# Cross attention in a decoder kernel: weighing last in the slot and two slots behind lowering, the first maximum folded, outputs in slots 8 and 10, the mean on ScalarE

## The chip, the cores and the metric

One core of a Trainium2 chip runs the whole program. The metric is the device time of one execution in microseconds, the median over runs. The engines are called as in the profile: PE (TensorE matmuls), PEld (its weight loads), DVE (VectorE), ACT (ScalarE), POOL (GpSimd), SP (SyncE).

## The reference

The program is a two-layer decoder. The change is in one of its six parts, the cross attention of layer 1, and that part computes, for 4 rows (batch entries) of 256 tokens:

```python
q = rms_norm((x @ Wq.T) as 16 heads of 128, q_norm_w)             # 256 queries
kv_in = concat([context (1601), x (256)])
k = rms_norm((kv_in @ Wk.T) as 4 heads of 128, k_norm_w)
v = (kv_in @ Wv.T) as 4 heads of 128
q, k = rope(q, positions of x), rope(k, all positions)
probs = softmax(q @ k.T / sqrt(128))                               # 4 query heads share a key head
x = x + (probs @ v) @ Wo.T
```

The norm is `w * (x * rsqrt(mean(x*x) + 1e-6))`. The mean in it, the maximum in the softmax and the product of the probabilities with v are what the change moves.

## The kernel before, in words

`cross_attention` prepares the normed tokens and constants (stage cross_w) and then calls `cross_stream`, in which every engine walks through the same list of numbered **slots** (`SLOTS`, L1755) and in each slot issues what an order written out by hand gives it. The engines meet only by semaphores, so an engine may run ahead or behind, and within an engine everything is in order.

The work has 4 rows x 4 key heads = 16 **groups**; each has 2 **passes** (half of the 4 query heads that share the key head: 512 columns = 2 heads x 256 queries). A pass has `STEPS` = 15 **steps**, one for each tile of 128 keys (the last has 65). So there are 32 passes and 480 steps, and step s starts in slot s. A group is 30 slots. One step goes through these stages:

- slot s: PE `score` (L1947, three bf16 matmuls of high and low parts into bank 0 or 1), ACT `copy_scores` (L2036) into a tile in memory called a room, DVE `keep_most` (L2203 for the first tile of a pass, L2206 for the others), which keeps the running maximum `most`. `score` of step s waits for `keep_most` of step s-2, whose bank it reuses.
- at the end of a pass: PE `turn_most` (L1955) transposes the maxima into bank 6, DVE `take_top` (L2212) reduces them, PE `turn_top` (L1961) turns them, ACT `flatten` (L2076) negates, PE `spread` (L1968) spreads them over bank 7. They stand in slots 0, 1 and 2 of the next pass (`TOPS_LATE`, `FLAT_LATE`, `SPREAD_LATE`); take_top in slot 0.
- slot s+18 (`LOWER`): DVE `lower` (L2194) adds the negated maximum, ACT `exponent` (L2042) takes exp.
- slot s+19 (`WEIGH`): PE `weigh` (L1979, one fp32 matmul seen as two instructions) multiplies with v, directly behind the slot's score; POOL `accumulate` (L2133, L2136) adds up the row sums. The room is free after both. There are 21 rooms (`ROOMS`), and `copy_scores` waits for the weighing and the sum of step s-21.
- after a pass: ACT `att_high` (L2082) and, a slot later, DVE `att_low` (L2248) split the result; PE `sum_up` (L1986) sums over partitions into bank 6, DVE `invert` (L2254) takes the reciprocal; PE `project_out` (L2000) multiplies each of the pass's two heads with Wo into bank 6, and DVE `add_out` (L2265) adds to x.

Counted modulo 15, a pass's att_high is in slot 4, att_low and sum_up in slot 5, and the two outputs in slots 6 and 9. In the last pass both outputs stand in one slot and in other banks.

Beside the steps run the projections for the next group, in 96 **units**, one every 5 slots (`EVERY`): 2 query units (128 queries of 4 heads) and 4 key units (up to 4 tiles) a group. From a unit's start slot: PE `project` (L1892) in slots 0 to 3 (a query unit in 0 and 1); ACT `square` (L2052) and, for key units, `take_values` (L2060) in slots 2 and 4; DVE `rotate` (L2233, L2234) in slots 3 and 6, and behind it `vary` (L2240), which makes the mean of the squares plus 1e-6; POOL `add_up` (L2143) in slot 6 and `normalise` (L2149, L2154) in slot 7; PE `turn` (L1934) in slot 9 transposes into bank 6; ACT `high` (L2070) in that slot and DVE `low` (L2244) in the next split the result. Modulo 15, turns stand in slots 2, 7 and 12.

Bank 6 is shared by turn_most, turn_top, turn, sum_up and project_out, in the order of the slots; `bank6_before` (L1835) makes each wait for the semaphore of the one before it: the reducing, flattening, low part, reciprocal or add. 

In three groups (1, 5, 9) the angles of the next row are made: DVE L2313 to L2319 in six slots from slot 29 to slot 4, ACT `waves` (L1628 to L1630, with table loads) behind slot 11. Around groups 3, 7 and 11 the next row's context is split (ACT L2117, DVE L2323) and POOL makes tables (L1608, L1609). The others are called plain groups here.

## Time and profile before

| | us |
|---|---|
| median of 3 runs | 1730.97 |
| lowest and highest | 1723.27, 1736.09 |
| the profiled execution's own time | 1732.53 |
| its span, first to last instruction | 1730.7 |
| of it, scores of slot 0 to slot 479 | 460.1 to 1601.6 |

The granted clock over the span is 0.953 of full speed. Slots 0 to 479 are two thirds of the span. Busy time in the tables below is a union: matmuls are pipelined, and the next begins before the one before it has ended in the record.

### The profile page before, as it was taken

The page shows a single profiled execution, that of the slowest core. Times are in us where ns is not written, and L with a number is a line of the kernel's source. Part 1 is how long each engine was busy: PE and PEld are TensorE (multiplying, and loading weights), DVE is VectorE, ACT ScalarE, POOL GpSimd, SP SyncE. Part 2 cuts the span into 40 slices and gives each one's busy share as a digit, 9 for nine tenths or more (in the row PEclk, how much of TensorE's full clock was granted, in tenths as well). Part 3 has the DMA queues.
Part 4 walks back from the last instruction along what each step waited for, and adds up shares of the span by engine and source line. Part 5 has one row for each costly group of instructions (what it writes and reads, how often), then busy time and mean ns, then how long its engine had stood idle before and what let it go on. Part 6 is the DMA issues. An engine that isn't in the chain of part 4 may idle for free. (4 is left out here: it accounts for less than half of the span.)

```text
span 1730.7 us, 26027 instructions
## 1 busy us (share of the span) xinstructions
PE 1517.4 (88%) x8324; PEld 878.2 (51%) x8324; DVE 1338.3 (77%) x2706; ACT 1014.7 (59%) x2343; POOL 1147.3 (66%) x1068
## 2 busy tenths in 40 slices
PE   6597796766798999999899999989989999999697
PEld 5476464533454554545455454545545555454354
DVE  7875577878687888888788878878887888888554
ACT  3363564652566666666666666666656666666342
POOL 2363470132577789888688977867998777886542
PEclk9799798879899999999999999999999999999889
DMA  3000820010000001000000000000000000000010
GB/s 97 1 2 13 303 88 25 1 70 0 32 13 1 13 13 39 1 1 1 1 1 13 27 1 1 1 1 1 21 19 1 1 1 1 1 1 1 7 49 26
DMA packets 30945, 38.49 MB, mean 22 GB/s; under 512 B 4948, under 2 KB 26456, under 8 KB 30808
## 3 DMA queue, kind: packets, MB, share of 16 engines
q1 hardware_dynamic: 30808, 36.82, 6.6%
q8 instruction: 67, 1.10, 0.3%
q14 instruction: 70, 0.57, 0.1%
HBM read 35.76 MB, written 1.05 MB: 21 GB/s over the span
## 5 line engine op out<-in xcount | busy, mean ns | idle before, releaser
L2136 POOL TENSOR_TENSOR stream_acc<-stream_acc,stream_weights 128x512 f32<-128x512 f32 (+1 forms) x404 | 523.6, 1296 | 135.6 <-ACT stream_weights L2042 119.8
L1979 PE MATMUL stream_banks<-stream_weights,stream_v 128*128 128x512 f32 (+1 forms) x872 | 458.8, 610 | 37.3 <-ACT stream_weights L2042 36.3
L2036 ACT COPY stream_weights<-stream_banks 128x512 f32<-128x512 f32 (+1 forms) x436 | 256.5, 588 | 263.3 <-PE stream_banks L1947 260.1
L2206 DVE TENSOR_TENSOR stream_most<-stream_most,stream_banks 128x512 f32<-128x512 f32 x448 | 304.9, 681 | 79.4 <-ACT stream_weights L2036 71.9
L2042 ACT ACTIVATE stream_weights<-stream_weights 128x512 f32<-128x512 f32 (+1 forms) x436 | 277.0, 636 | 110.4 <-DVE stream_weights L2194 107.6
L2194 DVE TENSOR_TENSOR stream_weights<-stream_weights,stream_banks 128x512 f32<-128x512 f32 (+1 forms) x436 | 295.1, 679 | 3.2 <-PE stream_banks L1968 1.8
L1979 PEld LDWEIGHTS stream_banks<-stream_weights,stream_v 128*128 128x128 f32 (+1 forms) x872 | 159.1, 191 | 132.6 <-ACT stream_weights L2042 81.9
L1947 PE MATMUL stream_banks<-stream_q_t_hi,stream_k_t_hi 128*128 128x512 bf16 (+1 forms) x480 | 183.6, 383 | 9.9 <-DVE stream_most L2206 8.6
L1947 PE MATMUL stream_banks<-stream_q_t_lo,stream_k_t_hi 128*128 128x512 bf16 (+1 forms) x480 | 183.1, 381 | 0.0
L1947 PE MATMUL stream_banks<-stream_q_t_hi,stream_k_t_lo 128*128 128x512 bf16 (+1 forms) x480 | 183.0, 381 | 0.0
L2143 POOL TENSOR_TENSOR stream_by_cos<-stream_by_cos,stream_by_sin 128x256 f32<-128x256 f32 x192 | 135.0, 725 | 50.0 <-DVE stream_by_sin L2234 49.8
L2154 POOL TENSOR_TENSOR stream_normed<-stream_by_cos,stream_rms 128x512 f32<-128x512 f32 x96 | 96.9, 1009 | 7.5
L2052 ACT ACTIVATE stream_squares<-stream_banks 128x128 bf16<-128x128 f32 x368 | 95.8, 270 | 10.1 <-PE stream_banks L1892 10.1
L2149 POOL TENSOR_TENSOR stream_rms<-stream_var,cross_half 128x4 f32<-128x4 f32 x96 | 101.4, 1056 | 0.0
L1892 PEld LDWEIGHTS stream_banks<-early_w_kv_hi,row_in_t_hi 128*128 128x128 bf16 x416 | 39.3, 98 | 88.0 <-issue 85.1
L1892 PE MATMUL stream_banks<-early_w_kv_hi,row_in_t_hi 128*128 128x256 bf16 x416 | 79.6, 273 | 0.6 <-DVE stream_by_sin L2234 0.6
L1892 PE MATMUL stream_banks<-early_w_kv_hi,row_in_t_lo 128*128 128x256 bf16 x416 | 79.4, 273 | 0.0
L1892 PE MATMUL stream_banks<-early_w_kv_lo,row_in_t_hi 128*128 128x256 bf16 x416 | 79.4, 272 | 0.0
L2265 DVE SCALAR_TENSOR_TENSOR model_x<-stream_banks,stream_inv,model_x 128x256 f32<-128x256 f32 x128 | 55.9, 477 | 28.4 <-PE stream_banks L2000 28.4
L1947 PEld LDWEIGHTS stream_banks<-stream_q_t_hi,stream_k_t_lo 128*128 128x128 bf16 (+1 forms) x480 | 47.6, 99 | 57.1 <-issue 1.5
L1934 PE MATMUL stream_banks<-model_ident,stream_normed 128*128 128x128 f32 x368 | 59.0, 282 | 20.0 <-DVE model_x L2265 18.5
L2052 ACT ACTIVATION_READ_ACCUMULATOR stream_squares<-stream_banks 128x1 f32 x368 | 75.0, 204 | 0.0
(436 smaller groups left out, 3114.3 us busy)
## 6 DMA issues: line engine op xcount, KB each, us to landing
memory_raw_t<-in_ctx_t SPq DMA_DIRECT2D x4, 1601.0 KB, 9.0
memory_raw<-in_ctx SPq DMA_DIRECT2D x4, 1536.0 KB
row_ctx_t<-in_ctx_t SPq DMA_DIRECT2D x6, 512.0 KB, 3.6
early_raw<-in_L_xattn_Wq SPq DMA_DIRECT2D x4, 512.0 KB, 3.9
early_raw<-in_L_xattn_Wo SPq DMA_DIRECT2D x4, 512.0 KB, 3.9
row_ctx_t<-in_ctx_t SPq DMA_DIRECT2D x1, 1601.0 KB, 8.0
moe_raw_up<-in_L_ffn_wi SPq DMA_DIRECT2D x6, 256.0 KB, 4.3
model_x<-in_x SPq DMA_DIRECT2D x1, 1024.0 KB, 5.5
```

The lines of the kernel that those rows point to most:

```text
L1892: last = nc.tensor.matmul(out, rows, moving(two, c), start=(n == 0), stop=(n == 3 * DC - 1))
L1947: last = nc.tensor.matmul(ps[0:r, step % 2, :], k_t[one][:, t * P:t * P + r], q_t[two][:, g % 2, PAIR * n:PAIR * (n + 1), :], start=(one = ...
L1979: nc.tensor.matmul(ps[:, 2 + n, :], v[0:r, g % 2, t, :], room(step)[0:r], start=(t == 0), stop=(t == KT - 1)).then_inc(weighed, 1)
L2036: nc.scalar.copy(room(step)[0:r], ps[0:r, step % 2, :]).then_inc(copied, 1)
L2042: nc.scalar.activation(room(step)[0:r], room(step)[0:r], ACT.Exp, scale=SCALE).then_inc(p_ready, 1)
L2052: last = nc.scalar.activation(squares[:, h, :], heads[:, h - some.start, :], ACT.Square, accum_out=ss[:, u % 2, h:h + 1])
L2136: nc.gpsimd.tensor_tensor(acc[0:r, h % 2, :], acc[0:r, h % 2, :], room(step)[0:r], ALU.add).then_inc(acc_ready, 1)
L2143: last = nc.gpsimd.tensor_tensor(by_cos[:, u % 2, 0:n, to], by_cos[:, u % 2, 0:n, to], by_sin[:, u % 2, 0:n, of], ALU.add)
L2149: nc.gpsimd.tensor_tensor(rms[:, u % 2, 0:n], var[:, u % 2, 0:n], half[:, 0:n], ALU.pow).then_inc(rms_ready, 1)
L2154: nc.gpsimd.tensor_tensor(normed[:, 0:n], by_cos[:, u % 2, 0:n], bcast(rms[:, u % 2, 0:n], 2, HD), ALU.mult).then_inc(normed_ready, 1)
L2194: nc.vector.tensor_tensor(room(step)[0:r], room(step)[0:r], ps[0:r, 7, :], ALU.add).then_inc(lowered, 1)
L2206: nc.vector.tensor_tensor(most[0:r], most[0:r], ps[0:r, step % 2, :], ALU.max).then_inc(maxed, 1)
```

## The change

WEIGH goes from LOWER + 1 to LOWER + 2 and ROOMS from 21 to 22. The room is made by laying the small tiles ss, var, rms, inv and flat into the unused end of `ctx_t`. On PE, the projection moves ahead of the top's steps and the weighing to the slot's end. On DVE, the first maximum of a pass is taken together with the second, from the room of the first tile (`maxima` counts the semaphore), the score of the third tile waits for the copy instead of the maximum, and take_top moves one slot on and ahead of the slot's maximum. Outputs stand in slots 8 and 10 of a pass; att_high, att_low and the sum move one slot on with WEIGH. The mean moves from DVE to ACT.

```diff
 LOWER = STEPS + 3
-WEIGH = LOWER + 1
-ROOMS = 21
+WEIGH = LOWER + 2
+ROOMS = 22
 def rows_of(tile):
...
 SUM_LATE = ATT_LATE + 1
+OUT_LATE = 2 * STEPS + 8
 def outs_in(slot):
...
     for m in range(PAIR):
-        found += [(h, m) for h in pass_at(slot, SUM_LATE + (1, 4)[m]) if h < PASSES - 1]
+        found += [(h, m) for h in pass_at(slot, OUT_LATE + 2 * m) if h < PASSES - 1]
         found += [(h, m) for h in pass_at(slot, SUM_LATE + 1) if h == PASSES - 1]
...
+        eps = sb("eps", [P, 1])
...
+                    nc.gpsimd.memset(eps[:], 1e-6)
                 @block.scalar
...
         v = sb("v", [P, 2, KT, HD])
-        ss = sb("ss", [P, 2, 4])
-        var = sb("var", [P, 2, 4])
-        rms = sb("rms", [P, 2, 4])
         by_cos = sb("by_cos", [P, 2, 4, HD])
         by_sin = sb("by_sin", [P, 2, 4, HD])
-        flat = sb("flat", [4, P], BF16)
         acc = sb("acc", [P, 2, HALF])
-        inv = sb("inv", [P, REP * QT])
         att = [sb(f"att_{part}", [P, PAIR, SEQ], BF16) for part in ("hi", "lo")]
         spare = ctx_t[:].rearrange("p c n -> p (c n)")
+        ss, var, rms = (spare[:, DC * CTX + 8 * i - 64:DC * CTX + 8 * i - 56].rearrange("p (u n) -> p u n", u=2) for i in range(3))
+        inv = spare[:, DC * CTX - 8:DC * CTX]
+        flat = spare[0:4, DC * CTX - 128:DC * CTX - 64].bitcast(BF16)
         SPARE_ROOMS = DC * CTX // HALF - 4
...
             return h, h // HALVES, h % HALVES, t
+
+        def maxima(step):
+
+            return step - step // STEPS
         def room(step):
...
                         pe.wait_ge(lo_ready, UNITS * g + QT + t // 4 + 1)
-                    if step >= 2:
-                        pe.wait_ge(maxed, step - 1)
+                    if step >= 2 and (step - 2) % STEPS == 0:
+                        pe.wait_ge(copied, step - 1)
+                    elif step >= 2:
+                        pe.wait_ge(maxed, maxima(step - 2))
                     else:
...
                 def turn_most(h):
-                    pe.wait_ge(maxed, STEPS * (h + 1))
+                    pe.wait_ge(maxed, maxima(STEPS * (h + 1) - 1))
                     wait_bank6("tops", h)
...
                     for c in range(4):
-                        last = nc.tensor.matmul(ps[:, 7, c * P:(c + 1) * P], own[:, c, :], flat[:], start=True, stop=True)
+                        last = nc.tensor.matmul(ps[:, 7, c * P:(c + 1) * P], own[:, c, :], flat, start=True, stop=True)
                     last.then_inc(spread_ready, 1)
...
                         score(slot)
-                    if 0 <= slot - WEIGH < ALL:
-                        weigh(slot - WEIGH)
+                    for e in range(4):
+                        for u in units_at(slot, e):
+                            project(u, e)
                     for h in pass_at(slot, TOPS_LATE):
...
                         spread(h)
-                    for e in range(4):
-                        for u in units_at(slot, e):
-                            project(u, e)
                     for u in turns_in(slot):
...
                         project_out(h, m)
+                    if 0 <= slot - WEIGH < ALL:
+                        weigh(slot - WEIGH)
             @block.scalar
...
                     last.then_inc(squared, 1)
+                def vary(u, n):
+                    heads = slice(0, width(u))
+                    if u >= 2:
+                        ac.wait_ge(rms_ready, u - 1)
+                    ac.wait_ge(squared, part_at[(u, n)] + 1)
+                    nc.scalar.activation(var[:, u % 2, heads], ss[:, u % 2, heads], ACT.Identity, bias=eps[:, 0:1],
+                                         scale=1.0 / HD).then_inc(var_ready, 1)
+
                 def take_values(u, n):
...
                         ac.wait_ge(spread_ready, h)
-                    nc.scalar.mul(flat[:], ps[0:4, 6, 0:P], -1.0).then_inc(flat_ready, 1)
+                    nc.scalar.mul(flat, ps[0:4, 6, 0:P], -1.0).then_inc(flat_ready, 1)
                 def att_high(h):
...
                             take_values(u, 0)
+                        else:
+                            vary(u, 0)
                     for u in units_at(slot, 4):
...
                             take_values(u, 1)
+                            vary(u, 1)
                     for h in pass_at(slot, FLAT_LATE):
...
                     r = rows_of(t)
+                    if t == 0:
+                        return
                     ve.wait_ge(copied, step + 1)
-                    if t == 0:
+                    if t == 1:
                         if h >= 1:
                             ve.wait_ge(most_turned, h)
-                        nc.vector.tensor_copy(most[:], ps[:, step % 2, :]).then_inc(maxed, 1)
+                        nc.vector.tensor_tensor(most[:], room(step - 1), ps[:, step % 2, :], ALU.max).then_inc(maxed, 1)
                     else:
-                        ve.wait_ge(maxed, step)
+                        ve.wait_ge(maxed, maxima(step - 1))
                         nc.vector.tensor_tensor(most[0:r], most[0:r], ps[0:r, step % 2, :], ALU.max).then_inc(maxed, 1)
...
                     nc.vector.tensor_tensor(by_sin[:, u % 2, some], heads, tab[1], ALU.mult).then_inc(taken, 1)
-                def vary(u):
-                    n = width(u)
-                    if u >= 2:
-                        ve.wait_ge(rms_ready, u - 1)
-                    nc.vector.tensor_scalar(var[:, u % 2, 0:n], ss[:, u % 2, 0:n], 1.0 / HD, 1e-6, ALU.mult, ALU.add).then_inc(var_ready, 1)
-
                 def low(u):
...
                         rotate(u, 0)
-                        if unit(u)[1] < QT:
-                            vary(u)
                     for u in units_at(slot, 6):
...
                             rotate(u, 1)
-                            vary(u)
+                    for h in pass_at(slot, TOPS_LATE + 1):
+                        take_top(h)
                     if 0 <= slot < ALL:
                         keep_most(slot)
-                    for h in pass_at(slot, TOPS_LATE):
-                        take_top(h)
                     for h in pass_at(slot, SUM_LATE):
...
```

## Rows read from the trace of the kernel before

**Rows 1.** The page's first part: busy time by engine.

```profile
PE 1517.4 (88%) x8324; PEld 878.2 (51%) x8324; DVE 1338.3 (77%) x2706; ACT 1014.7 (59%) x2343; POOL 1147.3 (66%) x1068
```

**Rows 2.** Windows by group: length, busy time (count) per engine, clock, DMA.

```profile
460.00:593.00 133.00, 117.84 (x575) 63.76 (x574) 106.29 (x192) 88.59 (x231) 95.13 (x92) 0.97 0.03 9
...
1036.00:1107.00 71.00, 68.49 (x335) 37.65 (x334) 57.94 (x108) 45.66 (x124) 57.42 (x56) 1.00 0.00 1
1107.00:1187.00 80.00, 71.05 (x334) 38.46 (x333) 63.61 (x114) 51.18 (x129) 61.57 (x56) 0.96 0.00 1
...
1257.00:1333.00 76.00, 70.94 (x340) 38.44 (x338) 62.13 (x112) 46.69 (x126) 64.93 (x66) 0.98 0.04 11
...
1545.00:1602.00 57.00, 53.48 (x217) 25.45 (x216) 47.63 (x82) 37.71 (x73) 40.84 (x36) 1.00 0.00 1
```

**Rows 3.** Waits of PE, 600 to 1600 us: total us, times, longest.

```profile
PE stream_banks L1979 <- ACT stream_weights L2042: 25.4, 39, 4.0
PE stream_banks L1934 <- DVE model_x L2265: 17.3, 13, 2.0
```

**Rows 4.** Timeline, slots 0 and 1 of a plain group.

```profile
1035.56 0.38 PE L1947 MATMUL stream_banks<-stream_q_t_hi,stream_k_t_hi 128*128 128x512 bf16 x1
...
1036.41 0.58 ACT L2036 COPY stream_weights<-stream_banks 128x512 f32<-128x512 f32 x1 [1.05 <-PE stream_banks L1947]
...
1037.07 0.60 PE L1955 MATMUL stream_banks<-model_ident,stream_most 128*128 128x128 f32 x4
1037.42 0.27 ACT L2052 ACTIVATE stream_squares<-stream_banks 128x128 bf16<-128x128 f32 x1
...
1037.77 0.69 DVE L2203 COPY stream_most<-stream_banks 128x512 f32<-128x512 f32 x1 [1.41 <-PE stream_banks L1955]
...
1037.92 0.38 ACT L2060 COPY stream_v<-stream_banks 128x256 f32<-128x256 f32 x1
...
1038.16 0.38 PE L1947 MATMUL stream_banks<-stream_q_t_hi,stream_k_t_hi 128*128 128x512 bf16 x1
...
1039.57 0.42 DVE L2233 TENSOR_TENSOR stream_by_cos<-stream_banks,row_k_tab_cos 128x256 f32<-128x256 f32 x1
...
1039.76 0.22 PE L1961 MATMUL stream_banks<-model_ident_b,stream_top 128*4 128x128 bf16 x1
```

**Rows 5.** Timeline, slots 6 and 7 of that group.

```profile
1050.08 0.69 DVE L2233 TENSOR_TENSOR stream_by_cos<-stream_banks,row_q_tab_cos 128x512 f32<-128x512 f32 x1
...
1051.28 1.17 DVE L2240 TENSOR_SCALAR stream_var<-stream_ss 128x4 f32<-128x4 f32 x1
...
1052.97 0.86 DVE L2265 SCALAR_TENSOR_TENSOR model_x<-stream_banks,stream_inv,model_x 128x256 f32<-128x256 f32 x2
...
1053.98 0.52 PE L1934 MATMUL stream_banks<-model_ident,stream_normed 128*128 128x128 f32 x3 [1.07 <-DVE model_x L2265]
```

**Rows 6.** Timeline, slots 11 to 13 of a group that turns angles.

```profile
1138.56 1.28 ACT L1628 ACT_TABLE_LOAD   x1
...
1144.66 0.63 ACT L2042 ACTIVATE stream_weights<-stream_weights 128x512 f32<-128x512 f32 x1
...
1145.34 2.07 PE L1979 MATMUL stream_banks<-stream_weights,stream_v 128*128 128x512 f32 x2 [3.97 <-ACT stream_weights L2042]
```

**Rows 7.** One line's instructions: ns min/median/max, forms.

```profile
L2240 DVE TENSOR_SCALAR stream_var<-stream_ss x96: 153/160/1180, 445.5 to 1554.5; 128x4 f32<-128x4 f32 x80, 128x3 f32<-128x3 f32 x16
```

**Rows 8.** Groups by line: shapes, busy us, mean ns, idle before.

```profile
L2070 ACT CAST stream_k_t_hi<-stream_banks 128x512 bf16<-128x512 f32 x64 | 36.2, 565 | 2.4 <-PE stream_banks L1934 1.3
L2082 ACT CAST stream_att_hi<-stream_banks 128x512 bf16<-128x512 f32 x32 | 18.4, 575 | 3.0 <-PE stream_banks L1979 3.0
L2248 DVE TENSOR_TENSOR stream_att_lo<-stream_banks,stream_att_hi 128x512 bf16<-128x512 f32 x32 | 21.9, 684 | 4.9 <-ACT stream_att_hi L2082 4.9
...
L1671 ACT ACTIVATE cross_w_rs<-cross_w_rs 128x8 f32<-128x8 f32 x1 | 0.2, 209 | 0.0
L2254 DVE RECIPROCAL stream_inv<-stream_banks 128x4 f32<-128x4 f32 x32 | 5.8, 182 | 22.8 <-PE stream_banks L1986 22.8
```

More of the change, by code:

```diff
@@ L1702, in _, with cross_stream @@
                                                 own_t[0][:, :, tok], ALU.subtract)
-        cross_stream(nc, x, const, a, w, experts, w_q, w_kv, w_o, k_gain, q_gain, freq, ones, own, half, own_t, in_t, ctx_t,
+        cross_stream(nc, x, const, a, w, experts, w_q, w_kv, w_o, k_gain, q_gain, freq, ones, own, half, eps, own_t, in_t, ctx_t,
                      where, where_f, angle, turns, sin, k_tab, q_tab, kept["raw"])
-def cross_stream(nc, x, const, a, w, experts, w_q, w_kv, w_o, k_gain, q_gain, freq, ones, own, half, own_t, in_t, ctx_t,
+def cross_stream(nc, x, const, a, w, experts, w_q, w_kv, w_o, k_gain, q_gain, freq, ones, own, half, eps, own_t, in_t, ctx_t,
                  where, where_f, angle, turns, sin, k_tab, q_tab, raw):
```

## The prediction

> **What bounds the kernel now.** The page's engine totals come first: PE 88%, DVE 77%, POOL 66%, ACT 59% [rows 1]. The share of PE hides the stage that the change touches, so the second view is the table of windows, one for each group of 30 slots [rows 2]. A plain group (eight of groups 1 to 14; its windows are all like 1036 to 1107) takes 71.0 us and PE is busy in 68.49 of them. Groups 1, 5 and 9, in which the next row's angles are made, take 80 us with 71.05 busy; groups 3, 7 and 11, in which the next context is split, 76 with 70.94. So PE is the bound, and what can be won is its idle time. The third view, PE's waits from 600 to 1600 us, says where it is: 25.4 us before the weighing matmul for ACT's exponent, and 17.3 us, 13 times, before the turning transposes for DVE's add into x [rows 3].
>
> Idle time understates a stall. A score matmul is shown as 0.38 us long though the next starts 0.22 later, so each stall first swallows about 0.16 us of tail. In the timeline I took each slot's length less its matmuls at their steady pace. Of a plain group's 71.0 us that leaves 3.7: 1.25 in slot 7 (the turn waits for the add of the output in slot 6; 1.07 of it shows as idle [rows 5]), 0.25 in slot 8, 0.3, 1.1 and 0.7 in slots 11 to 13 (weighing waits for the exponent, the score for the maximum) and 0.1 in slot 2. Slots 14 to 29 lose nothing. The cause in slots 6 to 13 is DVE: query units cost it two full-width products, and then the mean of the squares, a 128x4 instruction whose median is 160 ns and whose longest is 1180 [rows 7]. In slot 6 it takes 1.17 [rows 5]; I found it at 0.9 to 1.2 for nearly all query units after the first four.
>
> The Trainium skill (SBUF — State Buffer, Who interferes with whom) says that a DVE tensor_scalar between SBUF tiles can need the port pair that it shares with GpSimd, and then blocks until GpSimd's instruction ends, while ScalarE never waits on anyone. The trace agrees: the 1.17 us instruction ends as POOL's sum does. By that rule the long means vanish on ACT; without it each could cost ACT up to the 1.18 of DVE, 2 us more for a group's two query units.
>
> **The change, part by part.** I work in one plain group, in us from a slot's start. Fixed points, from slots 0 and 1 [rows 4]: the copy of scores starts 0.85 after the score and ends at 1.43; two squares take 0.50; after the copy, the exponent and two squares, the values are copied from 2.36 to 2.74; first transpose of the maxima to DVE's start 0.70. DVE instructions of 0.68 follow each other at 0.60, and PE starts about 0.15 after the DVE result it needs (add's end 1053.83, turn 1053.98 [rows 5]). PE's steady pieces: score 0.65, weighing 0.86, projection 0.65, four transposes 0.44, output 0.65, row sums 0.81.
>
> 1. Weighing last and one slot later. The exponent is then done two slots ahead, so the waits of the weighing go in every plain slot. What is late next is the maximum that the score two slots on needs: its earliest end is 2.15 and it is wanted after two slots (3.0 at least). The 22nd tile keeps the copy's distance to the weighing and to POOL's sum that it reuses at two slots, so it costs nothing; POOL's sum also gets its exponent earlier.
>
> 2. The mean on ACT. DVE loses 1.15 twice a group and 0.16 four times. ACT gains six instructions; the nearest row, 128x8, has 209 ns [rows 8], so I take 0.2 each, 20 us over the stage on an engine that is 64% busy in a plain group. Bounds: below nothing can't be; above, the 1.18 of DVE's longest. The Trainium skill (ScalarE: Activation LUTs, What ACT_TABLE_LOAD costs) prices an instruction with a column as bias at 280 ns instead; by it the wait in slot 7 below grows by 0.07, 1 us over the stage.
>
> 3. First maximum folded. One 0.69 copy less on DVE in each of 32 passes; it also waited 1.41 for the transposes [rows 4]. With 2 this removes the stalls of slots 11 to 13: adding up DVE's queue from slot 6, the maximum of slot 11 ends 0.2 before score 13 asks for it, that of slot 12 over 1 before. Gain 2.1, and 0.1 in slot 2.
>
> 4. take_top now stands in slot 1, behind rotate. New wait: rotate needs the values, copied at 2.74, that is 0.15 into slot 1. It then takes 0.75 (its products start 0.34 apart, the second lasts 0.41), take_top starts at 3.45 and ends at 4.13, and turn_top can start at 4.3. PE is there at 3.25 in slot 1 (no projection) and at 3.9 in slot 16. Queued behind it on PE are the weighing and the next score, so it is paid: 1.05 and 0.35. Least nothing, if PE trails; at most 1.2 more each, if DVE also has an angle instruction in front.
>
> 5. Outputs in slots 8 and 10. The turn in slot 7 waits no longer for an add, saving 1.25 and the 0.25 after it. It now waits for the reciprocal behind the row sums of slot 6. Before that stand, on ACT from slot 5: copy, exponent, the attention cast (0.58, now in slot 5 [rows 8]), four squares, mean, which holds copy 6 until 3.6. On DVE: two products to 4.8, maximum 6 to 5.4, reciprocal (0.18 [rows 8]) to 5.5. PE is there at 4.5: new wait 1.15. The output in slot 8 follows the low part of turn 7 by 0.2 and does not wait. In slot 23 it does: in ACT's slot 22 stand two squares, values and the mean ahead of the high part (0.57 [rows 8]), which ends 1.5 into slot 23; the low part ends at 2.2, and PE is at the output at 1.3: new wait 0.95.
>
> Plain stalls: old 3.7 gone, new 1.05 + 0.35 + 1.15 + 0.95 = 3.5. Net -0.15 in each of 14 groups: -2 us. The four waits could each be nothing or twice as long: 3.5 a group either way, 49 us, the widest bound of all.
>
> 6. Angle groups. ACT is away for its table loads and three waves from 1138.56, and the next exponent starts at 1144.66; PE weighed only at 1145.34, after 3.97 idle [rows 6], and the granted clock of that window is 0.96 against 1.00 of a plain one [rows 2]. Now this weighing needs nothing from that slot. What is late is copy 12, 6.8 after slot 11 starts, so maximum 12 ends at 7.5 and score 14, due at 5.6, waits 1.9; score 15 waits 0.85. Old extra 5.9, new 2.8 with 0.8 for a clock that may fall again: -2.3. In slots 1 to 7, where DVE has about six angle instructions besides, old extra 2.8, new 1.3: about -2.7 with group 1, the longest, counted in. -5 in each of three groups: -15 us. From nothing (the wait only moves to the score) to -9 (all their excess over 71).
>
> 7. Context groups. The old extra of 4.4 sits in slots 2, 7 and 8, behind DVE's split of 1.6; the split of slot 0 now falls where DVE idles, that of slot 5 lengthens the wait in slot 7 by 1.3. I take off 1 more for POOL, which has tables to make besides. -2 each, -6 us; from 0 to -4.4 each.
>
> 8. First group: PE is idle 15.2 in 460 to 593, of which 9 belong to group 1; of the other 6, the first weighing's wait, with the shorter DVE queue, gives -2.5. Last group: 3.5 idle [rows 2], slots without projection, where weighing waits most: -2.5. One more weighing in the drain I set against a maximum turned earlier: 0, within 1.5 either way.
>
> Sum: -2 - 15 - 6 - 2.5 - 2.5 = -28. The profiled execution took 1732.53 (span 1730.7 and 1.8 around it): 1704.5. It lies 1.6 above the median of 1730.97, so 1703.
>
> **The rivals.** (a) The old waits go and the new ones are half as long, because ACT and DVE run ahead once the means are gone: 1.75 x 14 = 25 more, 1678. For it: slots 16 to 29 had slack everywhere. Against: the four waits are chains, not queues. (b) The long stalls of the row changes only move, from the weighing to the score: parts 6 and 7 nothing, 1703 + 21 = 1724, within 1%. For it: ACT's 6 us absence stays. Against: the score has two slots of reserve. (c) Slower: bank 6 changes hands through ACT with one slot less. If ACT holds each mean until its own squares are through, and the high part, the values and the next copy queue behind it, every new wait grows. At 2 us more for a group it eats the 28; at 3.3 more (0.8 on each wait, within the bound of 3.5) the time is 1703 + 46 = 1749. Against: ACT's 45.66 us in a plain group of 71. (d) The extra slot of weighing does nothing, since PE was bound by throughput: only parts 2 and 3 count, and the time is as in (b).
>
> **How the numbers follow.** A measurement of this kernel can tell about 1% (17 us) from no change. Forecast, 1690 to 1714: 0.45. (a): 0.18. (b) with (d): 0.24. (c): 0.13. Faster by over 1% is the forecast and (a): 0.63; within 1%: (b), (d) and the milder part of (c), 0.27; slower: 0.10. The range leaves out about a tenth on each side: 1676 to 1738.
>
> **What would show it.** In a plain group: PE's wait for the exponent near nothing; new PE waits for the top maxima (slots 1, 16), for the reciprocal at the turn (slot 7), for the low part at the output (slot 23), about 1 us each; DVE busy about 4 us less than its 57.94; the mean on ACT near 0.2 with no table load beside it; plain groups still at 70 to 71.5, angle groups at 75. Wrong if plain groups fall below 69 (a), if they rise above 73 (c), or if angle groups stay at 80 (b).

## The result and the profile after

The changed kernel takes 1703.81 us, median of 4 runs (1701.68 to 1704.56), against 1731.08 (1723.27 to 1736.09): a ratio of 0.9846, 95% interval 0.9813 to 0.9879. The forecast was 1703. So the time is right; whether its terms are is another matter, and most of what follows is about terms that were wrong and cancelled. One execution of the kernel before, timed with b_outs below, took 5358.82 us and is left out of the median there.

The page's first part answers to [rows 1] (some 110 matmul records are missing in this trace, so PE's busy time is a little low). DVE lost 56 us, ACT gained 15. In the plain window below DVE is busy 3.0 us less than before (54.90 for 57.94), where the forecast had about 4.

```profile
PE 1481.1 (87%) x8215; PEld 854.0 (50%) x8324; DVE 1282.7 (75%) x2578; ACT 1029.3 (60%) x2439; POOL 1146.3 (67%) x1069
```

The windows by group, for the same stretches as [rows 2]: groups 0 and 1, a plain one, one with angles, one with a context split, the last; and, as a sixth, the experts' stage. Columns as there.

```profile
460.00:588.00 128.00, 114.98 (x566) 60.85 (x574) 101.74 (x176) 90.15 (x240) 93.51 (x91) 0.99 0.03 9
1023.00:1094.00 71.00, 67.68 (x333) 36.65 (x337) 54.90 (x102) 46.65 (x131) 58.12 (x56) 1.00 0.00 1
1094.00:1170.00 76.00, 67.26 (x327) 36.00 (x331) 59.96 (x104) 52.09 (x135) 60.34 (x56) 1.00 0.00 1
1241.00:1314.00 73.00, 67.15 (x324) 35.65 (x329) 56.29 (x100) 46.83 (x131) 63.76 (x65) 1.00 0.04 12
1526.00:1581.00 55.00, 52.05 (x210) 25.09 (x212) 46.05 (x79) 37.30 (x74) 42.39 (x38) 1.00 0.00 1
1618.00:1702.80 84.80, 72.07 (x424) 41.57 (x432) 46.57 (x126) 31.00 (x53) 28.22 (x25) 0.96 0.13 41
```

Windows have rounded ends. Measured from the score copy that opens one group to the one that opens the next, the plain groups before took 70.5 to 71.5 us and now take 70.5 or 70.6 (forecast -0.15 each, measured -0.3 on average). Groups 1, 5 and 9 fell from 80.5, 80.3 and 80.1 to 76.6, 76.3 and 76.2 (forecast -5, measured -3.9). Of the context groups, 7 and 11 fell by 1.8, and 3 did not (73.5 to 74.0; forecast -2 each). First and last group: -1.5 each (forecast -2.5). From the first score copy to the last that is 20.6 us, where the terms of the forecast give 28.

**PE's clock differed too.** Between the first score copy and the last, the kernel before ran for 30.7 us at the lower of the two clock levels (1.2 GHz of 2.4), all of it in groups 1, 5 and 9 (6.8 each) and 3, 7 and 11 (3.4 each); the changed kernel ran for 3.4 us at it, in group 1. That is the granted clock of 0.96 and 0.98 in [rows 2] against 1.00 above. In group 9 of the kernel before it fell at 1143.4, within the 3.97 us of idle time of [rows 6], and rose at 1150.2. What such a stretch costs can be read from groups 5 and 9, which run the same instructions. In the experiment u_mean below, group 5 had 6.8 us at the lower level and took 78.4 us, group 9 had none and took 76.5 (granted clock 0.96 and 1.00 in their windows):

```profile
795.50:873.90 78.40, 71.29 (x334) 37.13 (x333) 63.21 (x112) 51.27 (x130) 61.61 (x57) 0.96 0.00 1
1087.30:1163.80 76.50, 68.20 (x336) 36.14 (x334) 62.88 (x113) 51.21 (x130) 62.65 (x57) 1.00 0.00 1
```

Between the same two groups, 3.4 us more at the lower level go with 1.2 us more time in u_lag, with 0.5 in u_order and with none in o_top. By these (0 to 0.35 us for each us) the clock's share of the 20.6 can be anything up to 9.7 us; this is an estimate, and no run separates it.

PE's waits from 580 to 1580 us answer to [rows 3] (in this window the kernel before has 24.8 for the exponent, in 38 times, and 17.3 for the add): what PE waited for, us in total, times, longest. The waits for the exponent and for the add are gone, and three new ones stand in their place.

```profile
PE stream_banks L1968 <- DVE stream_top L2232: 20.4, 28, 1.4
PE stream_banks L1939 <- DVE row_ctx_t L2268: 15.7, 13, 1.7
PE stream_banks L2007 <- DVE stream_k_t_lo L2258: 11.2, 14, 1.2
PE stream_banks L1954 <- DVE stream_most L2226: 6.3, 5, 2.0
PE stream_banks L1939 <- POOL stream_normed L2172: 4.0, 6, 0.9
PE stream_banks L1975 <- DVE stream_weights L2212: 2.1, 2, 1.1
```

In the timeline of plain group 12 they are, in order, the top maxima in slot 1, the reciprocal at the turn of slot 7 (the place of the add in [rows 5]), the top maxima in slot 16 and the low part at the output of slot 23. The last column is the idle time: 1.03, 0.92, 0.27, 0.78, where the forecast had 1.05, 1.15, 0.35 and 0.95. The forecast counted a stall with the 0.16 us of tail that it swallows first; in that measure they are 1.19, 1.08, 0.43 and 0.94, together 3.6 for 3.5.

```profile
1317.79 0.22 PE L1968 MATMUL stream_banks<-model_ident_b,stream_top 128*4 128x128 bf16 x1 [1.03 <-DVE stream_top L2232]
...
1331.26 0.52 PE L1939 MATMUL stream_banks<-model_ident,stream_normed 128*128 128x128 f32 x3 [0.92 <-DVE row_ctx_t L2268]
...
1351.71 0.22 PE L1968 MATMUL stream_banks<-model_ident_b,stream_top 128*4 128x128 bf16 x1 [0.27 <-DVE stream_top L2232]
...
1368.98 0.28 PE L2007 MATMUL stream_banks<-cross_w_o_hi,stream_att_hi 128*128 128x256 bf16 x1 [0.78 <-DVE stream_k_t_lo L2258]
```

The mean on ACT, one line's instructions (ns min/median/max), against [rows 7]:

```profile
L2067 ACT ACTIVATE row_ctx_t<-row_ctx_t,cross_eps x96: 297/306/328, 443.6 to 1532.6; 128x4 f32<-128x4 f32 x80, 128x3 f32<-128x3 f32 x16
```

**Where the other 7 us are.** Span fell by 27.9, the stream's 480 slots by 20.6. From the last score copy to PE's last work of the stage it took 34.9 before and 31.5 now: -3.4, in the drain, which the forecast had at 0. And from the experts' first matmul to the end it took 87.8 and now 84.4, with no instruction changed there: -3.4 at a granted clock of 0.96 in the window above, against 0.90 in the kernel before in a window with the same 432 matmuls (it begins 2.9 us ahead of the first):

```profile
1640.00:1730.70 90.70, 76.84 (x432) 43.28 (x432) 47.42 (x137) 32.48 (x55) 28.19 (x25) 0.90 0.13 39
```

### The profile page after: what moved, and what is told of

Read it like the earlier page. It is cut to its first block and busy times, and to the rows that moved or that the text cites. A ratio compares the mean times of both kernels' runs of the same rounds, so it can differ in the third digit from the quotient of the medians.

```text
span 1702.8 us, 25942 instructions
## 1 busy us (share of the span) xinstructions
PE 1481.1 (87%) x8215; PEld 854.0 (50%) x8324; DVE 1282.7 (75%) x2578; ACT 1029.3 (60%) x2439; POOL 1146.3 (67%) x1069
## 3 DMA queue, kind: packets, MB, share of 16 engines
HBM read 35.76 MB, written 1.05 MB: 22 GB/s over the span
## 5 line engine op out<-in xcount | busy, mean ns | idle before, releaser
L1986 PE MATMUL stream_banks<-stream_weights,stream_v 128*128 128x512 f32 (+1 forms) x876 | 452.0, 600 | 0.0
L2226 DVE TENSOR_TENSOR stream_most<-stream_most,stream_banks 128x512 f32<-128x512 f32 (+1 forms) x416 | 283.9, 683 | 160.4 <-ACT stream_weights L2043 143.9
L1954 PE MATMUL stream_banks<-stream_q_t_hi,stream_k_t_hi 128*128 128x512 bf16 (+1 forms) x390 | 148.0, 379 | 10.2 <-DVE stream_most L2226 10.0
L1986 PEld LDWEIGHTS stream_banks<-stream_weights,stream_v 128*128 128x128 f32 (+1 forms) x876 | 139.7, 191 | 22.9 <-issue 5.3
L1954 PEld LDWEIGHTS stream_banks<-stream_q_t_lo,stream_k_t_hi 128*128 128x128 bf16 (+1 forms) x480 | 47.4, 99 | 148.0 <-issue 145.8
L1954 PEld LDWEIGHTS stream_banks<-stream_q_t_hi,stream_k_t_hi 128*128 128x128 bf16 (+1 forms) x480 | 47.3, 99 | 132.0 <-issue 96.7
L2172 POOL TENSOR_TENSOR stream_normed<-stream_by_cos,row_ctx_t 128x512 f32<-128x512 f32 x96 | 100.1, 1043 | 7.5
L2167 POOL TENSOR_TENSOR row_ctx_t<-row_ctx_t,cross_half 128x4 f32<-128x4 f32 x96 | 95.4, 993 | 0.0
L2253 DVE TENSOR_TENSOR stream_by_cos<-stream_banks,row_k_tab_cos 128x256 f32<-128x256 f32 (+1 forms) x128 | 51.4, 402 | 40.1 <-ACT stream_squares L2059 25.1
```

The source lines that it names most:

```text
L1954: last = nc.tensor.matmul(ps[0:r, step % 2, :], k_t[one][:, t * P:t * P + r], q_t[two][:, g % 2, PAIR * n:PAIR * (n + 1), :], start=(one = ...
L1986: nc.tensor.matmul(ps[:, 2 + n, :], v[0:r, g % 2, t, :], room(step)[0:r], start=(t == 0), stop=(t == KT - 1)).then_inc(weighed, 1)
L2167: nc.gpsimd.tensor_tensor(rms[:, u % 2, 0:n], var[:, u % 2, 0:n], half[:, 0:n], ALU.pow).then_inc(rms_ready, 1)
L2172: nc.gpsimd.tensor_tensor(normed[:, 0:n], by_cos[:, u % 2, 0:n], bcast(rms[:, u % 2, 0:n], 2, HD), ALU.mult).then_inc(normed_ready, 1)
L2226: nc.vector.tensor_tensor(most[0:r], most[0:r], ps[0:r, step % 2, :], ALU.max).then_inc(maxed, 1)
```

## The experiments

All were timed against the kernel before, whose medians lay between 1730.8 and 1732.2 in these sets. Six edits can be taken apart: PE's order, the lag with its tile, the mean, the fold, take_top's slot and the outputs' slots.

### First set: one part of the change undone

**u_mean**: the mean back on DVE, behind the products.

```diff
-                    ac.wait_ge(squared, part_at[(u, n)] + 1)
-                    nc.scalar.activation(var[:, u % 2, heads], ss[:, u % 2, heads], ACT.Identity, bias=eps[:, 0:1],
+                    nc.vector.tensor_scalar(var[:, u % 2, 0:n], ss[:, u % 2, 0:n], 1.0 / HD, 1e-6, ALU.mult, ALU.add)
```

> The changed kernel with the mean back on DVE behind rotate, all else kept. Theory (chains of waits per slot): the mean of a query unit takes 1.15 us there again. In slot 7 the reciprocal comes 1.0 later, so the turn's wait grows from 1.2 to 2.2; the maximum of slot 11 ends 0.9 after score 13 asks for it; slot 23 wins 0.3 on ACT. +1.65 in each of 15 groups: about 1728 us. Rival (only the weighing's distance matters, DVE's queue is off the path): 1703 to 1707.

Measured: 1714.40 us, ratio 0.9907 (0.9890 to 0.9923). The mean's move is worth 10.6, in size between the theory and its rival. A plain group grows by 0.6: slot 13 by 0.62, slot 7 by 0.20, and slot 23 is 0.19 shorter. The theory took every query unit's mean at 1.15 us; back on DVE, 20 of the 96 means took over 0.6 us, where the kernel before had 34.

**u_lag**: one slot of lag and 21 rooms, weighing still last.

```diff
-WEIGH = LOWER + 2
-ROOMS = 22
+WEIGH = LOWER + 1
+ROOMS = 21
```

> The changed kernel with WEIGH = LOWER + 1 and ROOMS = 21, weighing still last in the slot. Theory: last in the slot, the weighing finds its exponent done in a plain group even one slot behind; angle groups lose about 1 us each. The cast of the attention and the row sums go back to slots 4 and 5, so the reciprocal is there before turn 7: that wait of 1.2 falls to 0, and the output in slot 8 waits 0.15. About -10 us in all: 1694. Rival (the distance of two slots is what brought the gain): the exponent's waits come back, 1718 to 1728.

Measured: 1705.43, ratio 0.9851 (0.9834 to 0.9867): no difference from the changed kernel (the intervals overlap), and neither the theory nor its rival. The trace shows two effects that cancel. Plain groups are shorter, 69.6 or 69.7 for 70.5, as the row sums fall one slot earlier and the turn of slot 7 finds the reciprocal done. Groups 1, 5 and 9 are longer by 1.7 to 3.3. PE's waits from 580 to 1580 us in u_lag: the reciprocal is absent, and the exponent is back three times: 4.11 us at 838.93 and at 1130.02, behind ACT's waves in groups 5 and 9, and 1.30 in the last group. Ahead of this window it is back in group 1 too, with 4.11 at 547.23.

```profile
PE stream_banks L1968 <- DVE stream_top L2232: 19.4, 27, 1.4
PE stream_banks L2007 <- DVE stream_k_t_lo L2258: 13.3, 19, 1.1
PE stream_banks L1986 <- ACT stream_weights L2049: 9.5, 3, 4.1
PE stream_banks L1939 <- POOL stream_normed L2172: 7.3, 11, 1.0
```

**u_order**: PE's old order (weighing behind the score, projections behind the spread); everything else as changed.

```diff
                         score(slot)
+                    if 0 <= slot - WEIGH < ALL:
+                        weigh(slot - WEIGH)
...
                         spread(h)
+                    for e in range(4):
+                        for u in units_at(slot, e):
+                            project(u, e)
```

> The changed kernel with PE's old order in a slot (weighing right behind the score, projection behind the top's steps), distance two kept. Theory: the exponent is done two slots ahead, so the weighing waits nowhere, and its 0.86 us now covers the waits behind it: turn_top in slots 1 and 16 (1.05 and 0.35 to 0.2 each), turn in slot 7 (1.2 to 0.3), output in slot 23 (0.95 to 0.1). -2.5 to -3 in each of 15 groups: about 1662 us. Rival (weighing last is a part of the gain, since it lets the score's followers start early): 1710 to 1730.

Measured: 1674.92, ratio 0.9679 (0.9663 to 0.9696). PE's new order, the first thing the change does, costs 29 us; the theory had 42. The three new waits shrink from 20.4, 15.7 and 11.2 to 8.9, 9.2 and 0.6. The edit moves the projections as well as the weighing. In slots 1 and 7 there is no projection, and in slot 23 it is ahead of the output in both orders, so in these three only the place of the weighing differs. PE's waits from 580 to 1580 in u_order (the 4.7 us for POOL's sum lie behind the last score, in the drain):

```profile
PE stream_banks L1939 <- DVE row_ctx_t L2268: 9.2, 11, 1.8
PE stream_banks L1968 <- DVE stream_top L2232: 8.9, 14, 1.4
PE stream_banks L1993 <- POOL stream_acc L2154: 4.7, 1, 4.7
...
PE stream_banks L2007 <- DVE stream_k_t_lo L2258: 0.6, 2, 0.4
```

Its timeline in slot 1 shows why: the score, then the weighing of 0.86, and behind it turn_top has only 0.18 left to wait, where it waited 1.03 when it stood right behind the score.

```profile
1293.98 0.38 PE L1954 MATMUL stream_banks<-stream_q_t_hi,stream_k_t_lo 128*128 128x512 bf16 x1
1294.19 1.02 PE L1986 MATMUL stream_banks<-stream_weights,stream_v 128*128 128x512 f32 x2
1295.39 0.22 PE L1968 MATMUL stream_banks<-model_ident_b,stream_top 128*4 128x128 bf16 x1 [0.18 <-DVE stream_top L2232]
```

**a_top**: take_top back in the slot of the transposes, behind the maximum.

```diff
-                    for h in pass_at(slot, TOPS_LATE + 1):
-                        take_top(h)
                     if 0 <= slot < ALL:
                         keep_most(slot)
+                    for h in pass_at(slot, TOPS_LATE):
+                        take_top(h)
```

> The changed kernel with take_top back in slot 0, behind where the maximum stands. Theory: it can start 2.0 after slot 0 begins, ends at 2.7, and turn_top, due at 3.25 and 3.9, waits no more: slot 1 shorter by 1.05, slot 16 by 0.35; spread then waits up to 0.5 in slot 2 for the last lowering. -0.9 in each of 15 groups: about 1690 us. Rival (these waits only move to the next slots, whose chain through ACT and DVE is as long): 1702 to 1705.

Measured: 1696.24, ratio 0.9805 (0.9787 to 0.9824): 7.6 less than the changed kernel. The 20.4 us of PE's wait for the top maxima are gone, and 11.6 us of a wait of the spread for the lowering have come (2.1 in the changed kernel). In a plain group slots 1 and 16 lose 0.99 and 0.33; slot 2 gains 0.29: -1.0, a little more than the theory's 0.9. The time misses the theory's 1690 by 6 in the groups with angles: groups 5 and 9 take 78.0 for 76.3, with a wait of 2.6 for the lowering in slot 2 and 6.8 us at the lower clock, where the changed kernel has none.

### Second set

**u_fold**: the first maximum as a copy of its own again, in the changed kernel.

```diff
-                    if t == 0:
-                        return
-                    if t == 1:
+                    if t == 0:
...
-                        nc.vector.tensor_tensor(most[:], room(step - 1), ps[:, step % 2, :], ALU.max).then_inc(maxed, 1)
+                        nc.vector.tensor_copy(most[:], ps[:, step % 2, :]).then_inc(maxed, 1)
```

> The changed kernel (1703.8) with the fold alone undone: the first maximum of each pass is again a copy of its own (0.69 us of DVE in each of 32 passes, behind PE's transposes of the maxima). Theory, from the forecast: DVE is behind after the query units, and the copy it no longer saves gives back part of the stalls of slots 11 to 14. With the mean back on DVE (u_mean) that stall was 0.6 to 0.8 us a group; the fold saves less of DVE's time per group in the same slots, so about 0.8 us x 14 = 11 us more, 1715. Rival, the copy is hidden (it ran while DVE waited for the transposes anyway, and the mean on ACT has already cleared slots 11 to 14): 1702 to 1706.

Measured: 1725.9, median of 10 runs, ratio 0.9972 (0.9956 to 0.9988). The fold is worth 22 us, twice what I thought and in another place: slots 11 to 14 stay as they were in plain groups, and the loss is in slots 1 and 16 (2.74 to 3.11 each), and in the groups with angles, which take 77.8 to 80.8 for 76.2 to 76.6 (groups 1 and 5, the long ones, with 6.8 and 10.2 us at the lower clock, group 9 with none). PE's wait for the top maxima goes from 20.4 to 35.0, longest 2.7. DVE's timeline in slots 0 and 1 has no gap between the copy and take_top (L2228): the copy waits 1.10 for the transposes, and lowering, both products and take_top queue behind it.

```profile
1328.47 0.69 DVE L2219 COPY stream_most<-stream_banks 128x512 f32<-128x512 f32 x1 [1.10 <-PE stream_banks L1960]
1329.08 0.68 DVE L2210 TENSOR_TENSOR stream_weights<-stream_weights,stream_banks 128x512 f32<-128x512 f32 x1
1329.67 0.42 DVE L2249 TENSOR_TENSOR stream_by_cos<-stream_banks,row_k_tab_cos 128x256 f32<-128x256 f32 x1
1330.01 0.41 DVE L2250 TENSOR_TENSOR stream_by_sin<-stream_banks,row_k_tab_sin 128x256 f32<-128x256 f32 x1
1330.34 0.68 DVE L2228 TENSOR_REDUCE stream_top<-stream_banks 128x4 bf16<-128x512 f32 x1
```

**a_outs**: outputs in slots 9 and 10.

```diff
-OUT_LATE = 2 * STEPS + 8
+OUT_LATE = 2 * STEPS + 9
...
-        found += [(h, m) for h in pass_at(slot, OUT_LATE + 2 * m) if h < PASSES - 1]
+        found += [(h, m) for h in pass_at(slot, OUT_LATE + m) if h < PASSES - 1]
```

> The changed kernel (1703.8) with the outputs in slots 9 and 10 instead of 8 and 10, so the second pass's first output stands in slot 24 instead of 23. Theory: PE's wait of 11.2 us in 14 times for the low part at the output of slot 23 goes, and nothing takes its place, as slot 24's output finds the low part long done: 1703.8 - 11 = 1693. In the trace that wait is near zero. Rival: two adds of the output in neighbouring slots put DVE behind, and the wait turns into one of the score for the maximum or of slot 11: 1702 to 1706.

Measured: 1692.9, ratio 0.9781 (0.9755 to 0.9807), as the theory says. The wait for the low part at the output is no longer among PE's waits; nearly every group between the first and the last loses 1.0 and nothing takes its place.

**o_top**: u_order and a_top together (both diffs above).

> The changed kernel with PE's old order (u_order, 1674.9) and, besides, take_top back in the slot of the transposes. Theory: the two edits add up only as far as u_order still waits for the top maxima, 8.9 us in 14 times; the spread takes back 0.3 a group: 1674.9 - 8.9 + 4 = 1670. Rival, the edits are independent and take_top gives the 7.6 it gave in the new order: 1667. Second rival, the wait only moves to the spread, since the old order leaves DVE's queue as it is: 1674 to 1676.

Measured: 1668.04 (1667.55 to 1668.33), ratio 0.9643 (0.9619 to 0.9668), between the theory and the first rival. It is the fastest of all kernels here, 63 us under the kernel before. A plain group is down to 67.2 us, and PE is busy in 66.85 of a window of 67 (with [rows 2]: 68.49 of 71.0):

```profile
1000.00:1067.00 67.00, 66.85 (x333) 37.91 (x332) 53.55 (x98) 46.22 (x129) 56.02 (x55) 1.00 0.00 1
```

**o_lag1**: u_order and u_lag together.

> The changed kernel with PE's old order and the old lag of one slot and 21 tiles: what is left of the change is the mean on ACT, the fold, outputs 8 and 10 and take_top in slot 1. Theory: in a plain group the exponent is now early enough through the shorter DVE queue, and the row sums fall in slot 5, so that the turn of slot 7 no longer waits for the reciprocal (u_lag showed 0.9 us a group from that): -0.9 x 11 = -10; the angle groups lose what the lag gave, 2 to 3 us each: +9. 1673 to 1676, as u_order. Rival, the lag is what removed the waits for the exponent: they come back as 20 of the 27 us that the kernel before showed: 1695.

Measured: 1699.53, ratio 0.9819 (0.9791 to 0.9847): the rival, and 4.5 beyond it. In PE's old order the second slot of lag is worth 24.6 us, in the new order 1.6. PE's first wait from 580 to 1580 is the exponent again, against 0.8 us in u_order:

```profile
PE stream_banks L1986 <- ACT stream_weights L2049: 21.0, 27, 4.5
```

### Third and fourth set: one part alone

**b_outs**: the kernel before with the outputs in slots 8 and 10 alone. **b_lag**: the same with the second slot of lag and the 22nd tile. **b_order**: b_outs with PE's new order. In all three the small tiles already lie in `ctx_t`, as in the changed kernel.

```diff
 b_outs, b_lag, b_order
-        found += [(h, m) for h in pass_at(slot, SUM_LATE + (1, 4)[m]) if h < PASSES - 1]
+        found += [(h, m) for h in pass_at(slot, OUT_LATE + 2 * m) if h < PASSES - 1]
 b_lag
-WEIGH = LOWER + 1
-ROOMS = 21
+WEIGH = LOWER + 2
+ROOMS = 22
 b_order
-                    if 0 <= slot - WEIGH < ALL:
-                        weigh(slot - WEIGH)
...
                         project_out(h, m)
+                    if 0 <= slot - WEIGH < ALL:
+                        weigh(slot - WEIGH)
```

> The kernel before (1731.4) with the outputs in slots 8 and 10 alone; lag, PE's order, mean, copy and take_top as before. Against b_lag (1682.8) it has one slot of lag less. Theory, the gain of b_lag is the sum of two: PE's wait of 17.3 us for the output's add at the turn of slot 7 goes here, with the 0.25 of a group behind it, about 18 to 20 us: 1712, and the other 29 are the lag's. Rival, the lag is worth only the 24.6 that stood between o_lag1 and u_order: 1707. Second rival, the outputs pay nothing with one slot of lag, since DVE's queue is as long and the weighing waits for the exponent instead: 1725 to 1731.

Measured: 1713.95, ratio 0.9904 (0.9877 to 0.9930): against the 1730.79 of this set the outputs are worth 16.8, near the theory. PE's wait for the add is gone; its waits for the exponent (28.9 us in 42 times) and of the score for the maximum (9.3) are 4 us longer each than in the kernel before.

> The kernel before (1731.4) with the second slot of lag and the 22nd tile, and the outputs in slots 8 and 10 that this needs; PE's order, the mean on DVE, the first maximum's copy and take_top in slot 0 as before. Theory, the lag pays by itself in the old order: between u_order and o_lag1 (both with mean and fold) it was worth 24.6, and the parts add up: 1674.9 + 10.6 (mean) + 22.1 (fold) - 6.9 (take_top) = 1700.7. Rival, the lag pays only once DVE's queue is short: without mean and fold the maximum is late too, the score waits where the weighing waited, and the time is 1715 or more. Third: the fold's 22 hangs on take_top in slot 1, and without it this kernel is at 1680 to 1690.

Measured: 1682.78, ratio 0.9726 (0.9690 to 0.9763): the third expectation. Outputs and lag alone give 49 of the 63 us of the best kernel. PE no longer waits for the exponent (1.2 us), and the score waits for the maximum instead, 13.1 us in 14 times. Mean and fold together add 14.7 to this (o_top), where undoing them one by one in the changed kernel cost 10.6 and 22.1.

> The kernel before (1731.4) with PE's new order (projections ahead, weighing last) and the outputs in slots 8 and 10, the lag still one slot; mean, copy of the first maximum and take_top as before. Theory, weighing last only costs once the exponent's wait is paid by either way: in this kernel it removes the exponent's waits as the lag would, and brings the new waits of the short transposes: parts added from the changed kernel, 1703.8 + 1.6 (lag) + 10.6 (mean) + 22.1 (fold) - 7.6 (take_top) = 1730.5, no change. Rival, the cost of 29 us of the new order stands by itself and nothing is won: 1755. Other rival, less work of DVE in the wrong place matters only with take_top in slot 1: 1708 to 1715.

Measured: 1710.01, ratio 0.9877 (0.9835 to 0.9918): the second rival's range; the theory, which added up parts measured around the changed kernel, was 20 us too high. Between b_outs (1713.95) and this there are 3.9 us, and the intervals overlap: with one slot of lag, weighing last does remove most of the exponent's waits (28.9 to 9.1), and its price takes nearly all of it back (spread 3.0 to 16.3, low part at the output 0.5 to 13.6).

**o_top_inv**: o_top with the reciprocal ahead of DVE's products and maximum.

```diff
+                    for h in pass_at(slot, SUM_LATE):
+                        invert(h)
                     for u in units_at(slot, 3):
                         rotate(u, 0)
...
-                    for h in pass_at(slot, SUM_LATE):
-                        invert(h)
```

> The best so far (o_top, 1668.0: old order, take_top in slot 0, all else as in the changed kernel) with the reciprocal of the row sums ahead of the two products and the maximum in DVE's slot. Theory: PE's 8.1 us in 13 waits for the reciprocal at the turn of slot 7 are its place in DVE's queue, so they go, and what is late next there is small: 1661. Rival, DVE then waits for the row sums with the products queued behind it, and the maximum is later by as much: 1666 to 1670.

Measured: 1682.78, ratio 0.9722 (0.9684 to 0.9761): 14.7 worse than o_top, worse than the rival too. The reciprocal's wait is gone from PE's list, as the theory said, but the score and the output now wait:

```profile
PE stream_banks L1954 <- DVE stream_most L2226: 14.9, 17, 2.1
PE stream_banks L2007 <- DVE stream_k_t_lo L2258: 12.6, 13, 1.0
```

DVE itself waits for the row sums 30.3 us in 24 times, where in o_top, in whose slots the products and the maximum came first, it was 12.1 in 12. DVE's waits from 580 to 1580 us, o_top_inv and then o_top:

```profile
DVE row_ctx_t L2268 <- PE stream_banks L1993: 30.3, 24, 2.0
```

```profile
DVE row_ctx_t L2268 <- PE stream_banks L1993: 12.1, 12, 5.4
```

## Why the forecast was right, and where it was not

The sum was right. What the parts are worth in it can be read along one chain of runs, each one step from its neighbour: outputs in slots 8 and 10 (kernel before to b_outs) -16.8, second slot of lag (to b_lag) -31.2, mean and fold (to o_top) -14.7, take_top in slot 1 (to u_order) +6.9, PE's new order (to the changed kernel) +28.9. The change is 63 us of gain and 36 of loss. In another sequence the parts have other sizes, as the steps below show. By its own steps:

1. **Weighing last and one slot later.** "The waits of the weighing go in every plain slot": right. The step failed in taking two edits as one and the order as free. They do the same thing: PE's waits for the exponent go from 28.9 to 1.2 by the lag alone (b_lag) and to 9.1 by the order alone (b_order). With the old order the lag is worth 24.6 us (o_lag1 to u_order), or 31.2 with mean, first maximum and take_top as before (b_outs to b_lag). With the weighing last it is worth 1.6, within the noise. The order's price of 29 us was in the forecast (as most of 3.5 us a group), but under other names: as the new waits of steps 4 and 5. Step 4 even says that PE is at turn_top at 3.25 and that the weighing is queued behind it. I took that as given, and did not ask what the wait would be with 0.86 us of weighing in front. That a wait is "paid" depends on PE's order.
2. **The mean.** 0.306 us on ACT, where I took 0.2 from the 128x8 instruction of [rows 8]. The Trainium skill (ScalarE: Activation LUTs, What ACT_TABLE_LOAD costs) gives 280 ns and 0.83 per element for one with a column as bias, 283 here; the trace is 8% above it, and the row I took (209 ns) is a third below the trace. The wait in slot 7 did not grow by it (0.92 for 1.15). The long instructions are gone: the longest on ACT is 328 ns, on DVE 1180 [rows 7]. That agrees with what the Trainium skill (SBUF — State Buffer, Who interferes with whom) says of ScalarE, that it never waits on anyone. Worth 10.6 in all.
3. **The fold.** Its 2.1 a group was to come from slots 11 to 13, together with the mean. In plain groups slots 11 to 14 run at their steady pace in the changed kernel, but also without the fold. Its own part is in slots 1 and 16, where the first copy delays take_top: 0.7 in a plain group, up to 4.5 where angles are made too. The part above plain groups goes with more time at the lower clock. Much of the 22 us looks like a repair of what moving take_top did: with take_top in slot 0 and PE's old order, mean and fold together bring 14.7 (b_lag to o_top). How much of that is the fold's was not tried.
4. **take_top.** The waits of 1.05 and 0.35 measured 1.03 and 0.27. Undoing it gave 7.6, though, and not the 20.4 of PE's list, since the spread in slot 2 then waits for its own lowering.
5. **Outputs.** The old wait of 1.25 went (b_outs: 16.8 us, with [rows 3] showing 17.3), the new ones of 1.15 and 0.95 measured 0.92 and 0.78 of idle time, 1.08 and 0.94 with the tail. One slot later the second is free (a_outs, -10.9).
6. **Angle groups.** -3.9 for -5. The stalls behind the waves were right: slot 14 takes 4.38 where its matmuls need 2.16, slot 15 3.43 for 2.60, that is 2.2 and 0.8 for the 1.9 and 0.85 of the forecast. The miss is in the first slots: over a plain group, the first ten slots of groups 5 and 9 lose 2.2 us now (1.3 in the forecast) and lost 3.65 before (2.8). The forecast's -2.7 there does not follow from its own 2.8 and 1.3 either; their difference of 1.5 would have made the term -3.8 in place of -5, and group 1 was only 0.3 to 0.5 us longer than the other two. And the forecast charged 0.8 for the clock, which in the changed kernel did not fall in groups 5 and 9 at all; how much of the -3.9 is the clock's is open. With the new order, this is the one place where the second slot of lag pays.
7. **Context groups.** Groups 7 and 11 gave 1.8 of 2; group 3 got 0.5 longer. All three had 3.4 us less at the lower clock. The forecast took 4.4 us over a plain group for all three, but group 3 had only 2.5. The turn in slot 7 now waits 1.68, 0.76 more than in a plain group (forecast 1.3 more), and all three groups have a new wait in slot 12, for POOL's `normalise` (this one from group 11):

```profile
1271.01 0.66 PE L1939 MATMUL stream_banks<-model_ident,stream_normed 128*128 128x128 f32 x4 [0.92 <-POOL stream_normed L2172]
```

8. **Ends.** -1.5 for -2.5 twice. The drain gave 3.4 where I had 0; b_outs, o_lag1 and the kernel before, which have the old order and one slot of lag, have the long drain (34.8, 34.3 and 34.9 us), all others, which have the new order or the lag of two, 31.5 to 31.8. The experts' 3.4 go with the clock (the last section has the times) and were in no term.

So within the 480 slots the terms were 7 us too high (3 in step 6, 3 in step 7, 2 in step 8, less 1 in the plain groups), and the drain and the experts gave back 7 that no term held. That part of the agreement is luck. Of the rivals, (a) fell with the four waits at 3.6 of 3.5 a group, and (b) with the angle groups at 76 where it had 80. (c) did not come: none of the four waits grew beyond the forecast by more than 0.14. (d) was half right, and the forecast did not see that: the extra slot of weighing does next to nothing in the change (1.6 us), but because the weighing stands last, not because PE was bound by throughput, since in the old order it is worth 24.6.

## What to carry to other kernels

Two edits that give a result more time (consumed a slot later; consumed at the end of the slot) are one cure: take the cheaper one (here the lag, for one tile of memory), and measure them apart. An engine's filler, work whose operands are long ready, belongs ahead of its short instructions that wait for a chain through other engines; moved behind them, here it exposed three such chains and cost 29 us of 1704. When a forecast lists new waits, ask of each what stood in front of the waiting instruction in the old order, and price the order by their sum. And before an effect is put down to instructions, compare the time at the lower clock in the two traces: between these kernels it differed by 27 us in the stage that was changed.

## What was not expected of the hardware

The experts' stage is the same in all kernels here and did not take the same time. From its first matmul to the end it took 87.8 to 88.0 us in four of the profiled executions (before, u_order, a_outs, o_lag1) and 84.4 to 85.4 in the other ten. In the four, the clock was granted at its lower level of 1.2 GHz for 16.1 to 16.3 us of the stage, in the ten for 5.9 to 10.3; the two windows in the section on the result show it as a granted clock of 0.90 against 0.96. What sends an execution to the one or the other was not found, and no edit lines up with it. It is a step of 3 us, as large as the smallest effects above, and a profiled execution carries it into every difference of spans. In the 480 slots the same holds on a larger scale: there the profiled executions had between 0 (a_outs) and 41.0 us (b_order) at the lower level.
